# A layer's prologue, attention and last stage put into one block, with ScalarE's second gate moved behind the first transposed probabilities in each step

## What is computed

```
xn = layernorm(x)
qu, ku, vu, qc, kc, vc = split(xn @ W_qkv.T)              # 8 heads of 64 each
term1     = where(causal_mask, 0, (qc*s) @ vu.T)          # causal_mask: above the diagonal
lookahead = where(causal_mask, sigmoid((qu*s) @ ku.T), 0)
Su        = term1 @ lookahead.T
scores    = where(causal_mask, neg, (qc*s) @ kc.T - silu(Su))
attn_out  = (softmax(scores) @ vc) @ W_out.T
ffn_out   = (silu(xn @ wg.T) * (xn @ wu.T)) @ wd.T        # int32 weights / 127
out       = x + attn_out + ffn_out
```

## Time and profile before

| | us |
|---|---|
| median of 3 runs | 1185.25 (1185.08 to 1185.79) |
| the profiled execution | 1184.78 |
| its span, first to last instruction | 1183.0 |
| PE (TensorE) busy | 1105.5 (93%) |
| PEld (its weight loads) busy | 997.8 (84%) |
| DVE (VectorE) busy | 895.3 (76%) |
| ACT (ScalarE) busy | 772.9 (65%) |
| POOL (GpSimd) busy | 486.7 (41%) |

### The profile page before, as it was taken

The page is one execution under the profiler, slowest core; times in us unless marked ns, Lnnn a source line. Parts: engine busy times, 40 slices in busy tenths (PEclk is TensorE's granted clock), DMA queues, the critical chain, the costliest instruction groups (busy, mean ns, idle before and its releaser), DMA issues. The chain is left out here.

```text
span 1183.0 us, 21540 instructions
## 1 busy us (share of the span) xinstructions
PE 1105.5 (93%) x8000; PEld 997.8 (84%) x8000; DVE 895.3 (76%) x1866; ACT 772.9 (65%) x1387; POOL 486.7 (41%) x591
## 2 busy tenths in 40 slices
PE   4899999999999999999999999999999746999997
PEld 3788888888888888888888888888888745999997
DVE  5577788778877887787778777867787586878885
ACT  4577777777777777777777777777777653444443
POOL 0254456455544554555455545545554500000000
PEclk9999999999999999999999999999999877999999
DMA  4000000010010000000000000000000122243332
GB/s 142 1 1 10 28 10 14 11 32 10 10 27 11 10 9 28 10 10 10 28 9 11 10 28 10 10 11 28 10 10 11 45 71 82 93 139 112 103 117 64
DMA packets 29466, 41.00 MB, mean 35 GB/s; under 512 B 1456, under 2 KB 19120, under 8 KB 29360
## 3 DMA queue, kind: packets, MB, share of 16 engines
q1 hardware_dynamic: 29360, 39.59, 10.2%
HBM read 27.00 MB, written 12.58 MB: 33 GB/s over the span
## 5 line engine op out<-in xcount | busy, mean ns | idle before, releaser
L592 PE MATMUL X<-L_s,T_s 128*128 128x128 f32 (+3 forms) x1920 | 278.5, 303 | 5.7 <-issue 5.7
L592 PEld LDWEIGHTS X<-L_s,T_s 128*128 128x128 f32 x1920 | 266.6, 191 | 16.0 <-issue 5.9
L458 POOL TENSOR_SCALAR prob<-prob,inv 128x512 f32<-128x512 f32 (+1 forms) x248 | 265.7, 1090 | 9.5 <-DVE inv L907 9.5
L517 PE MATMUL X<-xT,W 128*128 128x512 f32 x960 | 236.5, 398 | 6.6 <-PEq L126 6.5
L517 PEld LDWEIGHTS X<-xT,W 128*128 128x128 f32 x960 | 178.0, 190 | 46.3 <-issue 7.1
L729 ACT ACTIVATE gate<-X 128x1024 f32<-128x1024 f32 (+1 forms) x96 | 84.8, 883 | 129.6 <-PE X L592 129.6
L883 DVE SCALAR_TENSOR_TENSOR gate<-gate,X 128x1024 f32<-128x1024 f32 (+1 forms) x96 | 99.5, 1038 | 75.8 <-ACT gate L729 75.8
L737 ACT ACTIVATE prob<-prob,least 128x512 f32<-128x512 f32 (+3 forms) x256 | 141.2, 562 | 6.7 <-DVE least L895 6.7
L448 POOL TENSOR_SCALAR_AFFINE_SELECT T_s<-T_s 128x512 fp32r<-128x512 f32 x128 | 112.5, 901 | 77.4 <-DVE T_s L876 77.4
L876 DVE TENSOR_TENSOR T_s<-X,T_s 128x1024 fp32r<-128x1024 f32 (+1 forms) x96 | 97.5, 1043 | 49.1 <-ACT T_s L715 49.0
L440 POOL TENSOR_SCALAR_AFFINE_SELECT tanh_l<-tanh_l 128x256 f32<-128x256 f32 (+1 forms) x96 | 46.4, 499 | 211.0 <-ACT tanh_l L707 210.8
(11 more groups left out here) (77 smaller groups left out, 1868.2 us busy)
## 6 DMA issues: line engine op xcount, KB each, us to landing
xb<-in_L_attn_x SPq DMA_DIRECT2D x16, 512.0 KB, 4.1
heads_out<-o_s SPq DMA_DIRECT2D x32, 256.0 KB, 2.2
f_o_in<-heads_out SPq DMA_DIRECT2D x8, 1024.0 KB, 5.7
f_xres<-in_L_attn_x SPq DMA_DIRECT2D x8, 512.0 KB, 4.8
out<-f_y SPq DMA_DIRECT2D x8, 512.0 KB, 3.2
w_raw<-in_L_attn_W_qkv SPq DMA_DIRECT2D x6, 512.0 KB, 6.8
tanh_l<-in_L_ffn_w_gate SPq DMA_DIRECT2D x1, 768.0 KB, 4.3
tanh_l<-in_L_ffn_w_up SPq DMA_DIRECT2D x1, 768.0 KB, 4.9
```

The lines of the kernel that those rows point to most:

```text
L458: last = pool.tensor_scalar(v, v, inv[:, h, w - 1:w], None, ALU.mult)
L517: last = pe.matmul(out, sh.W[:, a, k, cols], xT[:, c, k, :], start=(n == 0), stop=(n == 3 * KD - 1))
L592: last = pe.matmul(both[:, h, at:at + (J + 1) * P], T_s[:, h, a, to:to + P], L_s[:, h, c, WIDE[J + 1]:WIDE[J + 1] + (J + 1) * P], start=(J ...
```

## The change

The three functions become one, `layer`, with one block. Nothing that TensorE computes in attention's 32 steps changes, nor its order there.

- The prologue's work stands at the head of each engine's list. TensorE waits for each part of W by a semaphore of its own, and for x.
- W_qkv is loaded into pieces of tanh_l, gate and prob instead of a buffer of its own. Behind these loads SP copies the four weights of the last stage from DRAM to DRAM, in the layout in which they are used.
- In step 31 the weights of the last stage are loaded from these copies into the low half of their place, when the last projections are done. ScalarE and VectorE split them in that step, between their other work; the float conversion L846 is gone. The three maxima stand in VectorE's list of step 31 between low_PT 0 and silu_of 2.
- The tail behind step 31 is interleaved with the last stage's batch 0. TensorE does scores of pair 31 and attend of pair 30 (`drain`), reads has_low, does five gate and up groups, and then the transposes, the sixth group and the rest. The normalisation of pair 31 goes from VectorE (L941) to GpSimd. The buffers of the last stage are pieces of attention's.
- In each step ScalarE's list has high_PT 0 ahead of gate_of 1.

The core of the diff (whole new functions shortened):

```diff
             def step(part, b, q, g, back1, back2, ahead):
...
                 high_L(g, 1)
+                if part == LAST and q == 3:
+                    high_weights(0)
...
                 if back1:
                     exp_of(g - 1, 0)
+                if part == LAST and q == 3:
+                    high_weights(1)
...
                 high_L(g, 2)
+                if part == LAST and q == 3:
+                    high_weights(2)
...
+                if part == LAST and q == 3:
+                    high_weights(3)
...
                 gate_of(g, 0)
-                gate_of(g, 1)
                 if back1:
                     high_PT(g - 1, 0)
+                gate_of(g, 1)
                 gate_of(g, 2)
...
             def step(part, b, q, g, back1, back2, ahead):
...
                 low_L(g, 1)
                 if back1:
                     inverse(g - 1, 0)
                     minus_scores(g - 1, 2)
+                if part == LAST and q == 3:
+                    low_weights(0)
...
+                if part == LAST and q == 3:
+                    low_weights(1)
...
                 if back1:
                     inverse(g - 1, 1)
                 low_L(g, 2)
+                if part == LAST and q == 3:
+                    low_weights(2)
...
+                if part == LAST and q == 3:
+                    low_weights(3)
...
                 silu_of(g, 0)
                 silu_of(g, 1)
                 if back1:
                     low_PT(g - 1, 0)
+                if part == LAST and q == 3:
+                    take_low_max(0)
+                    take_low_max(1)
+                    take_low_max(2)
                 silu_of(g, 2)
...
+            def copy_weights():
+                for n, src in enumerate((w_gate, w_up, w_down, W_out)):
+                    to = w_copy[n].rearrange("p (n d) -> p n d", d=src.shape[1])
+                    sp.dma_start(to, src.rearrange("(n p) d -> p n d", p=P)).then_inc(w_copied[n], 16)
...
+            def drain():
+                g = LAST_G + 1
+                pe.wait_ge(PT_low, after(LAST_G - 1, 1))
+                pe.wait_ge(silu_done, after(LAST_G, 0))
+                scores(LAST, BATCH, 0, g, 0, double[2])
+                pe.wait_ge(PT_low, after(LAST_G - 1, 0))
+                scores(LAST, BATCH, 0, g, 1, double[0])
+                pe.wait_ge(silu_done, after(LAST_G, 2))
+                scores(LAST, BATCH, 0, g, 2, double[1])
+                pe.wait_ge(PT_low, after(LAST_G - 1, 2))
+                attend(LAST, BATCH, 0, g, double[3])
+
+            def ffn_first(products):
+                g = LAST_G + 1
+                pe.wait_ge(w_low, 2)
+                for m in range(5):
+                    gate_up(0, m, products)
+                pe.wait_ge(scores_emptied, after(LAST_G, 0))
+                turn_probs(LAST, BATCH, g, 0, double[2])
+                pe.wait_ge(o_copied, 2 * LAST_G)
+                turn_probs(LAST, BATCH, g, 1, double[3][:, 0, :])
+                gate_up(0, 5, products)
+                pe.wait_ge(hidden_done, 5)
+                turn_probs(LAST, BATCH, g, 2, double[0])
+                pe.wait_ge(w_low, 4)
+                down(0, 0, products)
+                down(0, 1, products)
+                attend(LAST, BATCH, 1, g + 1, double[3])
+                project_o(0, 0)
+                down(0, 2, products)
+                ffn_x(1)
+                project_o(0, 1)
...
+            turn_first_x()
+            pe.wait_ge(x_split, KD)
+            first_project(QU)
+            first_project(KU)
+            first_project(VU)
+            first_values()
+            first_project(QC)
+            first_project(KC)
             batches(lambda b, part: run_steps(b, part, step))
-            attend(LAST, BATCH, 0, LAST_G + 1)
-            scores(LAST, BATCH, 0, LAST_G + 1, 0)
...
+            drain()
+            pe.wait_ge(has_low_known, 1)
             has_low = pe.value_load(sh.has_low[0:1, 0:1], min_val=0, max_val=1)
```

More of the change, by code:

```diff
@@ L120, in scale @@
         last.then_inc(self.done, 1)
[L123 to L194, removed]
@@ new lines, in _ @@
+            for t in W_ORDER:
+                sp.dma_start(W_raw[t], W_qkv[:, t * INNER:(t + 1) * INNER].rearrange("(k p) c -> p k c", p=P)) \
+                  .then_inc(W_loaded[t], 16)
+            copy_weights()
+            batches(lambda b, part: run_steps(b, part, step))
+            sp.wait_ge(xT_low, BATCH * KD)
+            ffn_ln.load(sp, x, 1)
+            sp.wait_ge(L_ready, after(LAST_G, 2))
+            load_xres(0)
+            sp.wait_ge(low_max_taken, 3)
+            sp.dma_start(low_row[:, :], low_max[:, :]).then_inc(low_max_gathered, 16)
@@ L482, in _ @@
             mask_silu(LAST_G, 2)
+            for j in range(3):
+                norm(LAST_G, j)
+            batches(ffn)
         @block.tensor
@@ L563, in term1, with scores @@
                 last.then_inc(T_filled, 1)
[L565 removed]
+            def scores(part, b, q, g, j, both=None):
                 if j == 0:
@@ L677, in _, with turn_first_x @@
[L677 to L682, removed]
+            def turn_first_x():
+                pe.wait_ge(ident_ready, 1)
+                pe.wait_ge(first_ln.done, 1)
+                for k in range(KD):
+                    for n in range(TT):
+                        last = pe.transpose(double[0][:, k, n * P:(n + 1) * P], xb[:, n, k * P:(k + 1) * P], ident[:, :])
+                    last.then_inc(x_turned, 1)
@@ new lines, in first_project, with first_values, ffn_x @@
+            def first_project(t):
+                pe.wait_ge(W_split, W_ORDER.index(t) + 1)
+                project_into(bank("proj", t)[:, :], t, 0)
+            def first_values():
+                pe.wait_ge(W_split, W_ORDER.index(VC) + 1)
+                values_into(bank("V", 0), 0, 0)
+            def ffn_x(b):
+                pe.wait_ge(ffn_ln.done, b)
+                if b == 1:
+                    pe.wait_ge(o_copied, 2 * LAST_G + 2)
+                else:
+                    pe.wait_ge(fT_low, (b - 1) * KD)
+                for k in range(KD):
+                    for n in range(TT):
+                        last = pe.transpose(XT[k][:, n * P:(n + 1) * P], xb[:, n, k * P:(k + 1) * P], ident[:, :])
+                    last.then_inc(fT_filled, 1)
@@ new lines, in gate_up @@
+            def gate_up(b, m, products):
+                if b == 0 and m < 2:
+                    pe.wait_ge(scores_emptied, after(LAST_G, m + 1))
+                else:
+                    pe.wait_ge(hidden_done, b * HT + m - 1)
+                for bank, w in ((G[m % 2], sh.gate_w), (U[m % 2], sh.up_w)):
+                    n = 0
+                    for k in range(KD):
+                        for a, c in products:
+                            last = pe.matmul(bank, w[:, a, k, m * P:(m + 1) * P], xT[:, c, k, :],
+                                             start=(n == 0), stop=(n == len(products) * KD - 1))
+                            n += 1
+                last.then_inc(gu_filled, 1)
@@ new lines, in into_y @@
+            def into_y(parts, w, m, begin, end, products):
+                for t in range(TT):
+                    for n, (c, a) in enumerate(products):
+                        last = pe.matmul(Y[t // 2][:, (t % 2) * DIM:(t % 2 + 1) * DIM],
+                                         parts[a][:, m, t * P:(t + 1) * P], w[:, c, m, :],
+                                         start=(begin and n == 0 and t % 2 == 0), stop=(end and n == len(products) - 1),
+                                         skip_group_check=True)
+                    if end and t % 2 == 1:
+                        last.then_inc(y_filled, 1)
+                return last
@@ new lines, in _ @@
+            turn_first_x()
[6 more added lines that the diff above has]
+            first_project(KC)
+            batches(lambda b, part: run_steps(b, part, step))
+            drain()
+            pe.wait_ge(has_low_known, 1)
+            has_low = pe.value_load(sh.has_low[0:1, 0:1], min_val=0, max_val=1)
+            with pe.If(has_low == 0):
+                batches(lambda b, part: ffn(b, part, PRODUCTS[0:2]))
@@ L684, in _ @@
+            with pe.Else():
+                batches(lambda b, part: ffn(b, part, PRODUCTS))
         @block.scalar
@@ L802, in step @@
                     high_PT(g - 1, 2)
-                if part == LAST and q == 3:
-                    high_weights(0)
-                    high_weights(1)
+            high_W(QU)
+            high_W(KU)
+            high_first_x()
+            for t in (VU, VC, QC, KC):
+                high_W(t)
             for t in PROJ_ORDER:
```

767 lines of the change are left out of this document (386 added, 381 removed).

## The result

The changed kernel takes 1222.0 us (1221.0 to 1222.2, 4 runs) where the kernel before took 1185.2 beside it: a ratio of 1.031, interval 1.029 to 1.033. It is 3.1% slower. The prediction said 1221. Its own sum missed one wait and three sizes, though, and they are the subject of what follows.

What follows compares the result with a forecast made beforehand. TensorE was taken to bound attention, with VectorE's tail already on its path. 52.5 for the reordered steps, -5.1 prologue and -11.3 end gave +36.1: 1221 us, range 1210 to 1236.

Steps and rivals of the forecast that it cites:

- the 30 short pauses: Before each look-ahead in attention: pauses of 0.3 us listed as "issue", read as TensorE's wait for VectorE.
- The 1.75 us: End of steps 1 to 30: the late second gate delays VectorE's tail and TensorE's look-ahead by 1.75 us each, 52.5 altogether.
- the signs named: In attention: gate at least 0.9 us after transposes, VectorE's wait 1.75 longer, look-ahead waiting some 2, TensorE about 37 of 40.
- the three signs of being wrong: Look-ahead under half a microsecond after the last transpose; clock leaving 1.00 in mid-attention; first gate matmul under 10 us sooner.
- The prologue, -5.1: Kernel start: projections begin at 12.83 instead of 18.00, once x is split; -5.1 us, bounds -4 to -6.
- The end, -11.3: End of attention and first batch of the last stage, merged: -11.3 us, bounds -14 to -7.
- flag to matmul: Start of the last stage: from the flag to the first gate matmul, kept at 1.85 us.
- the first batch: Last stage, batch 0: 23.9 us before, plus 5.3 for moved-in work and 3 for waits of five gate-and-up groups.
- The clock: In attention: the new 1.85 us pause of TensorE was taken to cause no fall of the granted clock.
- Rival (a): In attention the clock falls too, 1.16 us each: 1233 at every third boundary, 1256 at all 30; chance 0.18.
- (b): Merged stages bring next to nothing, since maxima and flag hold TensorE as long as before: 1232 us; chance 0.05.
- (c): Faster: the look-ahead does not hang on VectorE's tail, so only the ends count: 1168 us; chance 0.05.

Runs made afterwards that it cites:

- the swap alone: The kernel before, with only ScalarE's high_PT 0 put ahead of gate_of 1, without the merge: 1242.1 us, ratio 1.048.
- the merge alone: The changed kernel with ScalarE's gate_of 1 put back ahead of high_PT 0: 1164.0 us, ratio 0.981; run again, 1165.5 us.
- the regrouped kernel: The kernel before with ScalarE's reordering, and transposed probabilities regrouped so only four transposes need the second product: 1249.6 us, ratio 1.055.
- both waits eased: The kernel before, reordered and with transposed probabilities regrouped, plus VectorE's first low half ahead of its second product: 1226.2 us, ratio 1.035.
- VectorE's low half first: The changed kernel with VectorE's low half of the first transposed probabilities ahead of its second product: 1226.2 us, ratio 1.034.

## Why the prediction was right, and where it was not

**What bounds.** Right: TensorE in attention, with no slack of VectorE's tail. All of the delay arrived. The reading of the 30 short pauses as the wait for VectorE was right for about half of each: with the banks freed early 0.18 of 0.34 us stayed.

**The 1.75 us.** Right in size, from the order of ScalarE's queue and the spacings of the earlier trace rows: 1.75 in the changed kernel, 1.76 with the swap alone, and nothing given back. Wrong in place. The step "TensorE, done at 920.72, starts the next step at 922.57" failed: TensorE was not done then, since its last eight transposes need banks 6 and 7 from the second product. Behind the second product both waits run on side by side, the low half with its 1.22 us and the eight transposes with their 1.09, and end within 0.01 us of each other, and so the sum came out. That is luck of durations, not a merit of the argument. It would have shown had the cure been derived from it: freeing banks 0 and 1 early, which the prediction's words suggest, brought nothing. Of the signs named, the late gate (0.96 us behind the transposes) and VectorE's longer wait (51.7 over 30, 1.72 a step) came. The look-ahead's "some 2 us, 30 times" did not (0.34), nor did TensorE fall to 37 of 40 (37.85). Two of the three signs of being wrong came too: the look-ahead starts 0.13 us after the last transpose (972.01 after 971.88), far less than half a microsecond, and the clock left 1.00 in mid-attention, twice. By its own signs the mechanism was in part wrong, though the time was right.

**The prologue, -5.1.** Measured -4.4. The projections start at 12.82 as forecast (12.83):

```profile
12.82 7.04 PE L544 MATMUL X<-xT,W 128*128 128x512 f32 x18 [1.44 <-DVE xT L1194]
...
25.55 0.97 PE L574 MATMUL X<-qu_s,ku_s 64*128 64x512 f32 x6 [1.50 <-DVE kc_s L1086]
```

The term mis-sized is what three of them take, 7.04 us for 6.26. Three or four are at work in each microsecond up to 19.00, some 6 us behind the first start; before, it was six from 22.00 on, 4 us behind it. It does not come with the merge as such. With the same prologue the merge alone took 5.98 and 5.92 us for them in its two profiles, which puts its mark of step 0 at 24.55 and 24.52, 5.4 us sooner than before. The term was right to within what executions differ by.

**The end, -11.3.** Measured -13.9. By the mark of step 31 (51.19 us later than before):

```profile
991.05 8.83 PE L620 MATMUL X<-L_s,T_s 128*128 128x512 f32 x48 [9.44 <-issue]
...
1005.06 5.06 DVE L1105 TENSOR_REDUCE low_max<-W 128x1 f32<-128x1536 f32 x3
...
1011.37 3.89 PE L604 MATMUL X<-kc_s,qc_s 64*128 64x512 f32 x24 [6.22 <-DVE PT_s L1171]
...
1017.87 0.14 DVE L1113 TENSOR_SCALAR has_low<-largest 1x1 int32<-1x1 f32 x1
...
1019.17 3.88 PE L734 MATMUL X<-xT,W 128*128 128x512 f32 x16 [1.21 <-issue]
```

```profile
1049.77 3.82 PE L734 MATMUL X<-xT,W 128*128 128x512 f32 x16
```

The sum starts at 939.86 in old times (forecast 939.6), the scores at 960.2 (960.3), the first gate matmul at 968.0 (969), the second batch's at 998.6 (1001.2); from there to the end it is 170.5 us, as before. So the splits and the three maxima (5.06) were well sized. Two terms were too dear: flag to matmul 1.30 and not 1.85 (no block ends in between now, which is likely the reason, but was not tested), and the first batch 30.6 and not 32.2.

**The clock.** The forecast took no fall; there were two in 30 boundaries. One of them, just behind the look-ahead of a step:

```profile
202.39 1.28 PE L574 MATMUL X<-qu_s,ku_s 64*128 64x512 f32 x6
...
203.40 3.01 PE L588 MATMUL X<-qc_s,vu_s 64*128 64x512 f32 x18
```

```profile
200.00:205.00 5.00, 3.71 (x22) 3.30 (x24) 4.57 (x5) 2.90 (x5) 1.11 (x3) 0.78 0.00 0
```

Term1's 18 matmuls take 3.01 us for 1.71, and the step is 1.6 longer than its like. The term was 1.16 a fall, from projection matmuls. Rival (a) was right in kind, at one boundary in fifteen. The rule of the Trainium skill named there ("TensorE: Matmul & The Clock Gate", "A second HAM failure mode: psum-queue depth-cycling") is borne out to that extent: with pauses in each step the changed kernel had falls, seldom, and none showed in mid-attention in the profile of before.

**The rivals.** (b) falls: the merge earned 18 us in the changed kernel and 21 by itself. (c) falls by the swap alone.

## What to carry to other kernels

In an in-order queue, an instruction put ahead of another hands on its own wait: ask what the one that is moved forward waits for, not only what it costs. The swap moved a 1.02 us eviction and cost 1.75, since the eviction was not ready. Look up every bank that the bottleneck takes in the stretch, before saying where it will stand; two waits that end together show up as one, and easing only one did nothing here. And a merge of stages whose gain is hidden behind a bad order can be worth more than the change as a whole shows: here 21 us, 28 with its own new pauses removed.

## What was not expected of the hardware

The clock's falls in attention are few, and their number differs from kernel to kernel: two in 30 boundaries in the changed kernel, one with the swap alone, three with the swap in 15 of them, two in the regrouped kernel, none in that with both waits eased, and four with VectorE's low half first, all of these before 150 us and the first of them in step 1. The five profiles of kernels without the swap have none from step 2 to step 30. Each is from one execution, so how the number depends on the pauses stays open. The two profiles of the merge alone differ in the first two steps by 1.5 and 1.4 us (24.5 and 28.1 us in one, 26.0 and 29.5 in the other), with the clock at 1.2 GHz for longer in the second. So single profiles of one kernel can differ by 3 us through the clock at the start alone. An activation with an int32 source took what the float one did: 1.47 us for 1536 columns in the changed kernel, 1.49 with a float source before.
